# Second attention stage: query projection, reciprocals, P V and output placed on other rounds

## The reference, cut to what matters

```python
q = (q_c @ w_qb).reshape(b, s, NH, QK).transpose(0, 2, 1, 3)
q_nope, q_rope = (q[..., :ND], q[..., ND:])
q_rope = q_rope * cos + rotate_half(q_rope) * sin
scores = jnp.einsum('bhqd,bhkd->bhqk', query, key_s) * scaling
attn = jax.nn.softmax(scores, axis=-1)
out = jnp.einsum('bhqk,bhkd->bhqd', attn, v)
return out @ w_o
```

## Time and profile before

| | |
|---|---|
| median of 3 runs | 1062.76 us (1059.85 to 1064.47) |
| the profiled execution | 1062.04 us, span 1060.2 us |
| first maximum of the stage to its last | 402.71 to 962.91 us of the span |
| busy over the span | PE 82%, PEld 53%, DVE 73%, ACT 50%, POOL 49% |
| mean granted clock of TensorE | 0.927 of full speed |

### The profile page before, as it was taken

The page is one execution under the profiler, slowest core; times in us unless marked ns, Lnnn a source line. Parts: engine busy times, 40 slices in busy tenths (PEclk is TensorE's granted clock), DMA queues, the critical chain, the costliest instruction groups (busy, mean ns, idle before and its releaser), DMA issues. The chain is left out here.

```text
span 1060.2 us, 15006 instructions
## 1 busy us (share of the span) xinstructions
PE 870.1 (82%) x4504; PEld 556.7 (53%) x4504; DVE 772.3 (73%) x1583; ACT 530.1 (50%) x1142; POOL 522.7 (49%) x449
## 2 busy tenths in 40 slices
PE   7488884799977955899998989997989898985477
PEld 1367763666666733455545555554455555553145
DVE  0669997734545535798999899999899999984353
ACT  1377773622214724455555555654555565553143
POOL 2043332011120006678778877885878877873003
PEclk9789987699998977699999999998999999999679
DMA  9420000800005760445555555553555555555101
GB/s 330 163 102 2 2 2 1 288 1 1 1 9 218 259 169 3 115 115 122 125 120 124 125 122 123 122 127 92 118 123 123 126 124 122 125 127 132 55 10 70
DMA packets 73105, 112.29 MB, mean 106 GB/s; under 512 B 18816, under 2 KB 23936, under 8 KB 72768
## 3 DMA queue, kind: packets, MB, share of 16 engines
q1 hardware_dynamic: 60736, 94.54, 32.3%
q10 hardware_dynamic: 12288, 16.79, 6.6%
HBM read 42.06 MB, written 2.10 MB: 42 GB/s over the span
## 5 line engine op out<-in xcount | busy, mean ns | idle before, releaser
L1334 DVE TENSOR_REDUCE nmax<-bank 128x1 f32<-128x512 f32 x256 | 173.9, 679 | 55.6 <-PE bank L1274 53.5
L1409 ACT ACTIVATE prob<-bank,nmax 128x512 f32<-128x512 f32 x172 | 118.5, 689 | 171.1 <-DVE nmax L1334 171.1
L1468 POOL TENSOR_TENSOR prob<-prob,rinv 128x512 f32<-128x512 f32 x129 | 133.7, 1044 | 51.7 <-DVE rinv L1341 51.7
L1349 DVE STREAM_TRANSPOSE blk<-prob 128x512 f32<-128x512 f32 x172 | 120.8, 703 | 3.1 <-ACT prob L1424 0.4
L1272 PE MATMUL bank<-xk_hi,q_hi 128*128 128x512 f32 x256 | 110.5, 432 | 14.7 <-ACT prob L1409 11.7
L1463 POOL TENSOR_TENSOR q_lo<-stage_a,q_hi 128x512 fp32r<-128x512 f32 x64 | 82.3, 1286 | 54.1 <-ACT q_hi L1403 54.1
L1273 PE MATMUL bank<-xk_lo,q_hi 128*128 128x512 f32 x256 | 103.0, 402 | 0.0
L1274 PE MATMUL bank<-xk_hi,q_lo 128*128 128x512 f32 x256 | 101.8, 398 | 0.0
L1409 ACT ACTIVATE stage_a<-bank,nmax 128x512 f32<-128x512 f32 x84 | 57.9, 689 | 75.5 <-DVE nmax L1334 75.5
L1272 PEld LDWEIGHTS bank<-xk_hi,q_hi 128*128 128x128 f32 x256 | 49.1, 192 | 78.7 <-issue 34.0
L1459 POOL TENSOR_TENSOR stage_a<-stage_a 128x512 f32<-128x512 f32 x64 | 82.8, 1293 | 6.3 <-DVE stage_a L1329 6.3
(11 more groups left out here) (214 smaller groups left out, 2155.5 us busy)
## 6 DMA issues: line engine op xcount, KB each, us to landing
pT<-blk SPq DMA_DIRECT2D x384, 64.0 KB, 2.0
raw_e<-blk SPq DMA_DIRECT2D x384, 64.0 KB, 2.0
wmod<-in_wmod SPq DMA_DIRECT2D x12, 1024.0 KB, 11.9
raw_e<-in_wo SPq DMA_DIRECT2D x8, 1024.0 KB, 6.3
pT<-blk ACTq DMA_DIRECT2D x128, 64.0 KB, 2.2
raw_e<-blk ACTq DMA_DIRECT2D x128, 64.0 KB, 2.1
wqn<-in_wqn SPq DMA_DIRECT2D x8, 512.0 KB, 4.0
stage_a<-in_wqkv SPq DMA_DIRECT2D x4, 768.0 KB, 8.9
```

Of the source, the lines that this page charges most:

```text
L1334: dve.tensor_reduce(nmax[:, s % RING:s % RING + 1], s_bank[s % 2][:, :], AX.X, ALU.max, negate=True).then_inc(max_done, 1)
L1349: dve.transpose(blk[:, u % T_SLOTS, :, :, 32 * st:32 * st + 32].rearrange("p j k q -> p k j q"), prob[s % RING]).then_inc(blk_done, 1)
L1409: act.activation(prob[s % RING], s_bank[s % 2][:, :], ACT.Exp, bias=nmax[:, s % RING:s % RING + 1], accum_out=rsum[:, s % RING:s % RING + ...
L1468: pool.tensor_tensor(prob[s % RING], prob[s % RING], bc(rinv[:, s % RING:s % RING + 1], [P, S]), ALU.mult).then_inc(norm_pool, 1)
```

## The change

PE, DVE, ACT and POOL get other rounds for the same work, and the reciprocals are made in pairs.

- `project` is on r1 and r5 instead of r0 and r4; the rotary parts are on r2, r3, r4 and r6, r7, r0; `q_sum`, `q_round` and `q_rest` follow one round later.
- `context` is on r2 and r3 instead of r1 and r3, `project_out` on r6 and r7 instead of r5 and r7; the splitting of its input on ACT and DVE is one round later (r4, r5), and so are `weights` and `out_weights`.
- One reciprocal instruction takes two columns, on every even round, for the two rounds before it; `normalize` and the ACT copy are one round later, and `TURN_LAG` is 4 instead of 3. 128 of 256 reciprocals go; nothing else is removed or added.

```diff
-            TURN_LAG = 3
+            TURN_LAG = 4
             MOVE_LAG = TPB + TURN_LAG
-            PV_AT = {1: (0, 1), 3: (2, 3)}
-            OUT_AT = {5: (0, 1), 7: (2, 3)}
+            PV_AT = {2: (0, 1), 3: (2, 3)}
+            OUT_AT = {6: (0, 1), 7: (2, 3)}
...
-                        if s % TPB == 0 and s // TPB + 2 < UNITS:
+                        if s % TPB == 1 and s // TPB + 2 < UNITS:
                             project(s // TPB + 2)
...
                     def row_inv(s):
-                        dve.wait_ge(exp_done, s + 1)
-                        if s >= RING:
-                            norm_ready(dve, s - RING)
-                        dve.reciprocal(rinv[:, s % RING:s % RING + 1], rsum[:, s % RING:s % RING + 1]).then_inc(rinv_done, 1)
+                        dve.wait_ge(exp_done, s + 2)
+                        for n in (s - RING, s + 1 - RING):
+                            if n >= 0:
+                                norm_ready(dve, n)
+                        dve.reciprocal(rinv[:, s % RING:s % RING + 2], rsum[:, s % RING:s % RING + 2]).then_inc(rinv_done, 1)
...
-                        if 1 <= s <= ROUNDS:
-                            row_inv(s - 1)
-                        if s % TPB and s // TPB + 2 < UNITS:
-                            rotate(s // TPB + 2, s % TPB - 1)
+                        if s % 2 == 0 and 2 <= s <= ROUNDS:
+                            row_inv(s - 2)
+                        if s >= 2 and (s - 2) % TPB < 3 and (s - 2) // TPB + 2 < UNITS:
+                            rotate((s - 2) // TPB + 2, (s - 2) % TPB)
...
-                        if s % 8 == 4 and 0 <= s // 8 - 2 < COUPLES:
+                        if s % 8 == 5 and 0 <= s // 8 - 2 < COUPLES:
...
-                        if st == 0 and u + 1 < UNITS:
+                        if st == 1 and u + 1 < UNITS:
                             q_round(u + 1)
-                        if st == (ACT_NORM + 2) % TPB and 1 <= u <= UNITS:
-                            n = s - 2
-                            act.wait_ge(rinv_done, n + 1)
+                        if st == (ACT_NORM + 3) % TPB and 1 <= u <= UNITS:
+                            n = s - 3
+                            act.wait_ge(rinv_done, n // 2 + 1)
...
-                        if 1 <= s <= ROUNDS and (s - 1) % TPB != ACT_NORM:
-                            normalize(s - 1)
-                        if st == 0 and u + 1 < UNITS:
+                        if 2 <= s < ROUNDS + 2 and (s - 2) % TPB != ACT_NORM:
+                            normalize(s - 2)
+                        if st == 1 and u + 1 < UNITS:
                             q_rest(u + 1)
...
-                        if st == 3 and u + 2 < UNITS:
-                            q_sum(u + 2)
+                        if st == 0 and 1 <= u < UNITS - 1:
+                            q_sum(u + 1)
```

More of the change, by code:

```diff
@@ L1407, in exps @@
                         ge(act, blk_done, s - RING + 1)
-                        ge(act, rinv_done, s - RING + 1)
+                        ge(act, rinv_done, (s - RING) // 2 + 1)
                         act.activation(prob[s % RING], s_bank[s % 2][:, :], ACT.Exp,
@@ L1432, in _ @@
                             weights(1)
-                        if s % 8 == 5 and s // 8 + 2 < COUPLES:
+                        if s % 8 == 6 and s // 8 + 2 < COUPLES:
                             weights(s // 8 + 2)
-                        if s % 8 == 0 and 0 <= s // 8 - 2 < COUPLES:
+                        if s % 8 == 1 and 0 <= s // 8 - 2 < COUPLES:
                             out_weights(s // 8 - 2)
-                        if s % 8 == 3 and 0 <= s // 8 - 2 < COUPLES:
+                        if s % 8 == 4 and 0 <= s // 8 - 2 < COUPLES:
                             j = s // 8 - 2
@@ L1466, in normalize @@
                     def normalize(s):
-                        pool.wait_ge(rinv_done, s + 1)
+                        pool.wait_ge(rinv_done, s // 2 + 1)
                         pool.tensor_tensor(prob[s % RING], prob[s % RING],
```

## The result

The changed kernel takes 1070.89 us (median of 7 runs, 1070.02 to 1073.04), the kernel before 1063.33 us beside it (7 runs, 1059.85 to 1067.25): ratio 1.0079, 95% interval 1.0055 to 1.0103. It is slower by 0.8%. The profiled execution's span is 1069.1 us, against 1060.2.

A forecast was written before the change was run, and what follows sets the result against it. DVE was taken to set the pace in most rounds and PE in some. Cycles +7.8 us, start -3.8 and end +2.2 gave +6.2, hence a forecast of 1069 us, range 1060 to 1076.

The forecast's parts named there:

- Two P V calls in a row: Half cycle r1 to r5: PE's 2.64 us behind the second call exceeds DVE's 2.26; +0.39 us a cycle.
- S(r4) = 3.46 + 2.64: Start of r4's scores on PE, counted from r1's maximum: r3's score start plus 2.64 us for scores and P V.
- Output calls and reciprocals: Half cycle from r5: second output call hidden by 0.1, two paired reciprocals saved on the chain; -0.12 us a cycle.
- The cycle: Eight rounds, two units: +0.27 us to 17.40, bounds +0.1 and +0.4; +7.8 us over some 28.75 cycles.
- The start: First rounds: round 1's scores come before the projection and `w_lo` ahead of `q_rest`; round 6's maximum 3.8 us earlier.
- The end: Last transfers: the turn lag moves unit 60's last transpose from r6 to r7, costing a round, +2.2 us.
- Without a break: SP issues the last four units' transfers with no pause, 48 in 31.4 us.
- At nothing: ACT copy, `normalize`, transposes, query chain, SP's issues and ACT's transfers stay covered and cost no time.
- The rival that DVE's occupancy speaks for: Second P V call hidden, DVE decides: chain -0.2 us a cycle, 1055 us, faster; chance 0.14.
- Rival 2: It cancels: chain grows by only 0.1 and the start gives 4 to 5 us, 1063 us; chance 0.18.
- Rival 3: `q_lo` late for r4's and r0's scores: 0.5 us for each of some 60 units, +30, 1098 us; chance 0.08.

The follow-up runs named there:

- e2: Kernel before with its second P V call moved from r3 to r2, right behind the first; 1078.72 us, ratio 1.0129.
- e7: Changed kernel with both P V calls one round later, on r3 and r4; 1042.02 us, ratio 0.9805.
- e4: Changed kernel with one reciprocal in each round again instead of pairs; 1077.13 us, ratio 1.0126.
- e3: Kernel before with its second output call moved from r7 to r6, right behind the first; 1063.80 us, ratio 0.9985.
- e6: Changed kernel with the turn lag back at 3 and the ACT copy one round earlier; 1071.15 us, ratio 1.0066.
- e5: Kernel before with only the change's start: unit 2's projection behind round 1's scores, second `w_lo` ahead of `q_rest`; 1060.45 us, ratio 0.9978.
- e8: Kernel of e7 with the output calls one round later too, on r7 and the next cycle's r0; 1034.88 us, ratio 0.9738.
- e10: Kernel before with only the change's two tables, P V on r2 and r3, output on r6 and r7; 1043.13 us, ratio 0.9795.
- e1: Changed kernel with the second P V call moved from r3 to r4, an empty round between the calls; 1053.58 us, ratio 0.9919.

## Why the prediction was right

The forecast was 1069, slower, by one wait; it came out at 1070.89, with that wait. The sum was less exact than this looks: it gave +6.2 us, and the two profiled executions differ by 8.9 us of span, the medians by 7.6; two effects that it didn't name, of over 2 us each, nearly cancel. By its own steps:

- **Two P V calls in a row, +0.39 a cycle: right in kind, too small.** The half cycle from r1 to r5 takes 713.53 - 704.39 = 9.14 us, forecast 9.01, before 8.62: +0.52. The step that was mis-sized is the second call's "S(r4) = 3.46 + 2.64". Scores that come behind a P V call take 0.89 us up to the next call (707.88 to 708.77) and not 0.79 (705.22 to 706.01): the first of the three matmuls lasts 0.50 and the second starts 0.34 behind it, not 0.23. I took 2.64 from a round whose scores did not stand behind a call. The same 0.50 and 0.34 show where PE had stood waiting (the projection at 713.04 and 713.38), so it isn't only the kind of matmul in front. e2 shows the same 2.76, and e7 that it costs nothing where PE has a lead.
- **Output calls and reciprocals, -0.12: right.** From r5 to the next r1: 717.83 - 713.53 = 4.30 us, then 2.19 and 1.89, 8.38 us; forecast 8.39, before 8.51. The two-column reciprocal lasts 0.15 us and the next instruction starts 0.07 behind it (712.25 to 712.32), the same as one column. e4 gives the pair's worth, 0.13 us a cycle; e3 that the output calls are hidden.
- **The cycle:** forecast 17.40, measured 17.51. Over 26 regular cycles (rounds 32 to 144 and 152 to 248) +9.82 us; the +7.8 I gave for 28.75 cycles would have been 10.9 at 0.38.
- **The start, -3.8:** -3.69 at round 6 (416.65 - 402.88 = 13.77 against 17.46). The projection started at 406.30 (forecast 406.1), round 2's maximum at 410.01 (409.8).
- **The end, +2.2:** +2.64. The first issue came 1.89 later against round 248's maximum. "Without a break" was wrong: SP paused 1.22 us before the last 24 issues (969.71 to 970.93), as it does in every cycle of the changed kernel, which I didn't see coming; e6, with the shorter lag, has one of 0.10 there.
- **Not forecast:** rounds 16 to 32, two cycles, took 1.71 us less where 0.76 more was due, and the stretch behind SP's last issue 2.09 us more. In the first the kernel before had rounds of 3.40 and 3.56 us where later cycles have 1.70 and 2.77, which is its whole excess of 2.49 us over two regular cycles; the changed kernel has none (35.04 for 2 x 17.51). TensorE's clock is the cause: from 443.41 to 446.81 us it was granted 0.50 in the kernel before (1.2 GHz), and from 439.85 to 448.00, the same rounds, 1.00 in the changed one. The P V call of that round, before and after:

```profile
446.70 2.74 PE L1285 MATMUL bank<-pT,c_all 128*64 128x512 f32 x8
...
443.37 1.94 PE L1285 MATMUL bank<-pT,c_all 128*64 128x512 f32 x8
```

This isn't the schedule's doing alone: such a slow round stands near round 16 in the profiles of the kernel before, e2, e3, e4, e5, e8 and e10, and in none of the other five. Why the clock is low there is not shown. In the second, the last P V ran 1.17 us longer at a lower granted clock; the other 0.92 is not traced. That the two nearly cancel is luck.
- **At nothing: right.** e6 shows it for POOL, ACT and the transposes, and from 470 to 970 us DVE waits for nothing but PE's scores.
- **A loose reading.** The 36.8 us of waits were called nearly all of the 9% in which DVE is idle; over the 500 us they are 7.4%. Nothing in the sum hangs on it.

The rival that DVE's occupancy speaks for (1055, faster) fell: DVE's share went down while the time went up. Under it lay a true reading, that removing the reciprocals and starting earlier are gains: with the P V call set apart they show (e1, 1053.58). Rival 2 (it cancels, 1063) fell with its premise: the cycle grew by 0.38 us, not 0.1. Rival 3 (the query is late) did not show: `q_lo` is done at 707.72 (706.45 + 1.27) and the scores that need it begin at 710.64, 2.9 us later, where 2.8 was forecast.

The rule of the Trainium skill, *Perfetto Trace Analysis*, Identifying the Most-Contended Engine, points at DVE alone here, while PE, with a weight-load share of 52%, set the pace of four maxima in eight (r2, r3, r4, r7). The advice of the Trainium skill, same page, Optimization Strategy, to look at the gaps on that engine and at what it waits for did lead to the right place; whether more buffers would close them, no run here shows.

## What to carry to other kernels

When two engines are both near 90% busy and one feeds the other through two buffers, judge a schedule by the round, not by the mean: write down for each round what either engine needs, and follow the longer one. A producer's long rounds should come when it has a lead, and an empty round belongs right behind the point where it was held up; the change and e8 do the same work and lie over 3% apart (1070.89 and 1034.88 us). Shifting everything together keeps the distances, so look at what did not shift: here the second P V call, one round nearer to the projection.

## What the runs showed of the hardware

- A rotary part on 32 partitions costs DVE more than one on 128 partitions, though they last 0.69 and 0.67 us. In the changed kernel the transpose starts 0.72 us behind part 1 (709.60 to 710.32) but 0.58 behind part 2 (703.18 to 703.76): the 128-partition operation overlaps its neighbour and the 32-partition one does not. With the starts before and behind it, a round of the kernel before with part 0 or 1 takes 2.26 us and one with part 2 1.90. In the kernel parts 0 and 1 also read and write at partitions 64 and 96, where the instructions around them start at partition 0, so these rows don't tell how many partitions from which ones. Why wasn't tried.
- A 128x128 matmul behind the 64-column ones of P V holds the next one up by 0.34 us instead of 0.23 (707.88 to 708.22), and the first P V matmul starts 0.32 behind the last 128x128 one (708.45 to 708.77): 0.1 us for each change from one kind to the other. The first matmul after a wait holds the next one up too, without such a change (704.00 to 704.30 and 713.04 to 713.38: 0.30 and 0.34).
- A reciprocal of one or of two columns takes the same 0.07 us of DVE's time from start to start (712.09 to 712.16 before, 712.25 to 712.32 after), about half of the duration shown.
- At a granted clock of 0.50 the projection's matmuls start 0.43 us apart instead of 0.23 (444.01 to 444.43 and 444.86 in the kernel before; 441.66 to 441.89 in the changed one).
